# A graph layer on one core: second-phase table picks from three bf16 parts in 25 quads of 56 steps, own projections kept in DRAM, and 32 steps of rows issued by SyncE

## What is computed

```python
h = jnp.maximum(_layernorm(x), 0.0)
feat = relu(h @ W_pool + b_pool)
w = edge_weight / segment_sum(edge_weight, dst)[dst]
neigh = segment_max(feat[src] * w[:, None], dst)
rst = h @ W1_self + neigh @ W1_neigh + b1
h1 = relu(rst / norm(rst))
neigh2 = segment_sum(h1[src] * w[:, None], dst) / deg[:, None]
out = x + relu(h1 @ W2_self + neigh2 @ W2_neigh + b2)
```

## Time and profile before

| | |
|---|---|
| median of 3 runs | 3998.56 us (3998.48 to 3999.13) |
| the profiled execution | 3995.4 us |
| its span, first to last instruction | 3993.7 us |
| POOL busy in the span | 2970.4 us (74%) |
| DVE busy | 3064.5 us (77%) |
| PE busy | 2828.0 us (71%) |
| ACT busy | 1384.0 us (35%) |
| first phase, first to last gather | 113.4 to 1882.9 us |
| second phase, first to last gather | 2030.4 to 3847.2 us |

### The profile page before, as it was taken

The page is one execution under the profiler, slowest core; times in us unless marked ns, Lnnn a source line. Parts: engine busy times, 40 slices in busy tenths (PEclk is TensorE's granted clock), DMA queues, the critical chain, the costliest instruction groups (busy, mean ns, idle before and its releaser), DMA issues. The chain is left out here.

```text
span 3993.7 us, 55758 instructions
## 1 busy us (share of the span) xinstructions
PE 2828.0 (71%) x8603; PEld 1440.9 (36%) x8603; DVE 3064.5 (77%) x5593; ACT 1384.0 (35%) x4000; POOL 2970.4 (74%) x3150
## 2 busy tenths in 40 slices
PE   3133332222199999993679999999999999998536
PEld 3033332212144444441434443334434343345324
DVE  6488888768589998884568888888889898874234
ACT  6344443333333333332433333333333333334310
POOL 7777777777767777776767777777777777777766
PEclk8555555555599999996579999999999999996555
DMA  7333334444433333333333333333333333333335
GB/s 207 92 108 111 114 115 129 128 128 118 138 119 111 121 120 112 115 117 109 98 92 117 114 115 116 115 119 110 114 117 111 121 110 121 110 107 106 116 115 149
DMA packets 226164, 469.73 MB, mean 118 GB/s; under 512 B 67234, under 2 KB 144164, under 8 KB 200964
## 3 DMA queue, kind: packets, MB, share of 16 engines
q0 software_dynamic: 100416, 205.90, 20.0%
q1 hardware_dynamic: 116676, 258.00, 18.0%
q10 hardware_dynamic: 8704, 2.25, 0.3%
HBM read 240.82 MB, written 225.06 MB: 117 GB/s over the span
## 5 line engine op out<-in xcount | busy, mean ns | idle before, releaser
L519 POOL DMA_INDIRECT G<-h_tab,SRC x1451 | 1369.2, 944 | 460.0 <-issue 322.4
L519 POOL DMA_INDIRECT G<-feat_tab,SRC x1399 | 1326.9, 948 | 443.9 <-issue 295.0
L867 DVE TENSOR_TENSOR CP<-pH,kc 128x1024 f32<-128x1024 f32 x1225 | 1494.3, 1220 | 113.0 <-PE pM L1025 61.0
L640 ACT ACTIVATE pT<-G,EW 128x128 f32<-128x128 f32 x1434 | 525.0, 370 | 1009.1 <-DMA G<-h_tab,SRC 340.6
L640 ACT ACTIVATE pM<-G,EW 128x128 f32<-128x128 f32 x1416 | 518.8, 371 | 1012.6 <-DMA G<-h_tab,SRC 319.8
L1000 PE MATMUL pH<-CP 128*128 128x98 bf16 x1563 | 144.3, 281 | 597.6 <-DVE CP L825 597.6
L1024 PE MATMUL pM<-CP,A 128*128 128x512 f32 x882 | 463.0, 607 | 63.0 <-DVE CP L867 60.8
L1025 PE MATMUL pM<-CP,A 128*128 128x512 f32 x882 | 454.6, 597 | 0.0
L810 DVE SCALAR_TENSOR_TENSOR S<-S,C,pT 128x128 f32<-128x128 f32 x782 | 269.8, 345 | 220.4 <-ACT pT L640 198.2
L1024 PE MATMUL pC<-CP,A 128*128 128x512 f32 x784 | 409.9, 605 | 38.4 <-DVE CP L867 36.9
L1025 PE MATMUL pC<-CP,A 128*128 128x512 f32 x784 | 404.1, 597 | 0.0
(11 more groups left out here) (149 smaller groups left out, 2896.2 us busy)
## 6 DMA issues: line engine op xcount, KB each, us to landing
scan<-S SPq DMA_DIRECT2D x97, 1032.0 KB
scan<-S SPq DMA_DIRECT2D x97, 1024.0 KB
GR<-feat_tab SPq DMA_DIRECT2D x3456, 0.5 KB
GR<-h_tab SPq DMA_DIRECT2D x3456, 0.5 KB
GA<-feat_tab ACTq DMA_DIRECT2D x2176, 0.5 KB
GA<-h_tab ACTq DMA_DIRECT2D x2176, 0.5 KB
G<-h_tab,SRC POOLq DMA_INDIRECT x1451
G<-feat_tab,SRC POOLq DMA_INDIRECT x1399
```

The lines of the kernel that those rows point to most:

```text
L519: pool.indirect_dma_start(out=dst, out_offset=None, in_=table, in_offset=bass.IndirectOffsetOnAxis(ap=idx, axis=0)).then_inc(s, 16)
L640: act.activation(scaled(t), v, ACT.Copy, scale=EW[:, t:t + 1]).then_inc(s_mul, 1)
L867: dve.tensor_tensor(OH[:, k % 2, :, :], pH[:, :].unsqueeze(1).to_broadcast([P, 2, 4 * P]), kc[:, 2 * j:2 * j + 2].unsqueeze(2).to_broadcas ...
```

## The change

- The second phase has 25 quads with windows of 56 steps, from step 76 on. The first phase keeps 8 quads with windows of 80 steps, one block later.
- For them the table is split at the start of the second phase into three bf16 parts, in 75 pieces, one in each of the steps 0 to 74: PE puts a group into PSUM, DVE rounds it to bf16, PE subtracts that part, and so on (`SPLIT`, `split`, `third`). Two parts take the place of the fp32 tile in A, the third lies in U and HL.
- A pick of the second phase is one DVE instruction with 1024 bf16 results (`pick_split`), compared with codes that are made once at the start and loaded as bf16, and six bf16 matmuls in place of two fp32 ones. Four one-hot buffers instead of two.
- The own projections run in the steps 120 to 1545. SP loads a group of `h_tab` (`load_nodes`), and stores the result to a new DRAM tensor (`store_own`); the last node stage reads it back (`load_own`).
- SP issues the rows of 32 steps in each phase, used one block later than before.

```diff
-QUADS = [(0, 54 + QB * i) for i in range(8)] + [(1, QB * i) for i in range(17)]
+SPL = 76
+Q1 = [(0, T * 55 + 80 * i, 80) for i in range(8)]
+Q2 = [(1, SPL + 56 * i, 56) for i in range(25)]
+QUADS = Q1 + Q2
+NHOT = 4
...
 def chunk_block(c):
-    return 7 * c // 16
+    return 3 * c // 8
...
-ROWT = [T * (chunk_block(CH * k + CH - 1) + 1) + 9 for k in range(27)]
+ROWT = [T * (chunk_block(CH * k + CH - 1) + 2) + 9 for k in range(32)]
...
+AHEAD = 16
+OWN_FIRST, OWN_EACH = 120, 57
+OWN = {OWN_FIRST + OWN_EACH * g: g for g in range(NGR + 1)}
...
+                    if phase:
+                        for g in range(NGR):
+                            if b == own_load_block(g):
+                                load_nodes(g)
+                            if b == own_store_block(g):
+                                store_own(g)
...
+            def pick_split(u, j, k):
+                if j == 0:
+                    arrived(dve, s_si, u)
+                    dve.wait_ge(s_o2, k)
+                    link(dve.tensor_copy(pH[:, :], SI[:, u % 2, :].bitcast(F32)))
+                dve.wait_ge(s_od, max(K1, k - NHOT + 1))
+                dve.tensor_scalar(HOT[:, k % NHOT, :], PH16[:, :], kcode[:, j:j + 1], None,
+                                  ALU.is_equal).then_inc(s_o2, 1)
...
+                    if phase:
+                        for i in range(2):
+                            hot = HOT[:, k % NHOT, 4 * P * i:4 * P * (i + 1)]
+                            v = 2 * j + i
+                            pe.matmul(picked(u), AB[:, v, 0, :], hot, start=(v == 0), stop=False)
+                            pe.matmul(picked(u), AB[:, v, 1, :], hot, start=False, stop=False)
+                            ins = pe.matmul(picked(u), low_tile(v), hot, start=False, stop=(v == NT - 1))
```

More of the change, by code:

```diff
@@ L43, in quad_mul @@
     return QUADS[u][0] * TS + quad_steps(u)[-1] + 1
-PICKS = {(phase, T * b + j * T * QB // NJ): [] for phase, b in QUADS for j in range(NJ)}
-for u, (phase, b) in enumerate(QUADS):
+PICKS = {(phase, t + j * n // NJ): [] for phase, t, n in QUADS for j in range(NJ)}
+for u, (phase, t, n) in enumerate(QUADS):
     for j in range(NJ):
[L49 to L52, removed]
+        PICKS[phase, t + j * n // NJ].append((u, j))
+STARTS = {(phase, t // T): u for u, (phase, t, n) in enumerate(QUADS)}
+TAKEN = {(phase, t + n + (3, 7)[phase]): u for u, (phase, t, n) in enumerate(QUADS)}
+READ = {(phase, t + n + (7, 11)[phase]): u for u, (phase, t, n) in enumerate(QUADS)}
+SPLIT = [(g, k) for r in range(0, NGR, 2) for k in range(3) for g in range(r, min(r + 2, NGR))]
+SPLIT_AT = {gk: n for n, gk in enumerate(SPLIT)}
+assert len(SPLIT) < SPL
 PAT = {(QUADS[u][0], t): (u, i) for u in range(QN) for i, t in enumerate(quad_steps(u))}
@@ L104 @@
 I32 = mybir.dt.int32
+TWO = 0x40000000
 U8 = mybir.dt.uint8
@@ L122, in hist_of, with own_load_block, own_store_block @@
     return [k for k in (2 * (b - H0), 2 * (b - H0) + 1) if 0 <= k < NB]
[L125 to L135, removed]
+AHEAD = 16
+OWN_FIRST, OWN_EACH = 120, 57
+OWN = {OWN_FIRST + OWN_EACH * g: g for g in range(NGR + 1)}
+assert max(OWN) + AHEAD < TS and OWN_FIRST > len(SPLIT) + AHEAD
+def own_load_block(g):
+    return (OWN_FIRST + OWN_EACH * g - AHEAD) // T - 2
+def own_store_block(g):
+    return (OWN_FIRST + OWN_EACH * (g + 1)) // T + 1
 def build(nc, x, src, srcq, srcr, dstx, ew, w_pool, b_pool, w1s, w1n, b1, w2s, w2n, b2, out):
@@ L142, in build @@
     scan2 = nc.dram_tensor("scan2", (EP, D), F32).ap()
+    owntab = nc.dram_tensor("own_tab", (NP, D), F32).ap()
+    codes = nc.dram_tensor("codes", (QN, 8 * P), BF16).ap()
     with ExitStack() as ctx:
@@ L320, in build @@
         s_pq = sem("s_pq")
+        s_qi = sem("s_qi")
+        s_qe = sem("s_qe")
+        s_qs = sem("s_qs")
+        s_sp = sem("s_sp")
+        s_sd = sem("s_sd")
+        s_ring = [sem(f"s_ring{i}") for i in range(3)]
+        s_os = [sem(f"s_os{i}") for i in range(3)]
         s_ost = [sem(f"s_ost{i}") for i in range(3)]
@@ L421, in _ @@
                 sp.dma_start(rows(feat, g), F[:, g % 3, 0:len(tiles_of(g)), :]).then_inc(s_fst[g % 3], 16)
+            sp.wait_ge(s_qe, 1)
+            sp.dma_start(codes, QB[0:QN, :]).then_inc(s_qs, 16)
             ahead = []
@@ L449, in store_blocks @@
                             load_feat(i)
-                    if (phase, b) == (0, QUADS[0][1] - 1):
+                    if (phase, b) == (0, QUADS[0][1] // T - 2):
                         load_sources(0)
@@ L942, in _ @@
                 combine(1, t)
+                if t < len(SPLIT):
+                    split(t)
                 for u, j in PICKS.get((1, t), ()):
@@ L1091, in project_own @@
                 ins.then_inc(s_qp, 1)
+            for n, (g, k) in enumerate(SPLIT):
+                o = in_quad(pR[g % 2], len(tiles_of(g)))
+                if k:
+                    pe.wait_ge(s_sd, SPLIT_AT[g, k - 1] + 1)
+                    pe.matmul(o, nident[:, :], third(g, k - 1), start=False, stop=True,
+                              skip_group_check=True).then_inc(s_sp, 1)
+                else:
+                    if g >= 2:
+                        pe.wait_ge(s_sd, SPLIT_AT[g - 2, 2] + 1)
+                    pe.matmul(o, ident[:, :], raw(g), start=True, stop=True).then_inc(s_sp, 1)
+            pe.wait_ge(s_sd, len(SPLIT))
             for t in range(TS):
```

97 lines of the change are left out of this document (82 added, 15 removed).

## The result

The changed kernel takes 4219.48 us, median of 4 runs (4218.37 to 4220.38), beside 3998.52 for the one before (3995.79 to 3999.13). The ratio is 1.0554, with an interval of 1.0536 to 1.0572: 5.5% slower. The profiled execution took 4219.15 us with a span of 4217.4.

A forecast was written before the change was run, and what follows sets the result against it. The prediction took POOL's gathers, 1.25 us each, to bound the kernel before, with SP taking over after the change. 3995.4 + 121 (first phase) + 103 (second phase) + 1 (last stage) = 4220 us, range 4150 to 4290.

The forecast's parts named there:

- The mechanism: Both phases: added rows raise SP to 19.3 us a block, above POOL's 17.8 and 18.1, so SP sets the pace; 0.82.
- The first phase: Blocks 1 to 95, 63 of three chunks and 32 of two, plus loads, on SP: phase ends near 2008 us, +121 us.
- The second phase: From its start, 60 three-chunk and 30 two-chunk blocks plus code loads and own transfers on SP: 1924 us, +103 us.
- The 0.8 for each own transfer: Second phase, SP's queue: 50 transfers of own groups at 0.8 us each, 40 us, bounds 20 and 55.
- The last stage: After the second phase: SP loads 25 more groups of 256 KB beside the last gathers, 1 us (0 to 5).
- DVE: Second-phase picks: a comparison takes 0.68 us, so a 56-step window needs 53 us of DVE under SP's 70.
- The rival of 250 us more: Second phase: DVE's comparisons run at one element a cycle, a window takes 80 us, not 70; time 4470 us; chance 0.04.
- PE: Second-phase picks: six matmuls take 1.28 us, a window 66.5 of 70 us, leaving PE 5% away from being the bound.
- Rival 1: POOL stays the bound, kernel faster at 3935 us; needs SP's second-phase block under 18.1 us, a chunk 7% cheaper; chance 0.06.
- Signs in the profile: Expected after: hardly any SP waits, blocks of 21.6 and 14.8 us, POOL waiting for ACT 100 us or more, comparisons 0.65-0.7 us.
- Rival 1's 17 us: First phase: up to 17 us of POOL stalls that the later use of the rows could remove, counted in Rival 1's time.
- The register loads: SP's loads of 16 offsets: costed at the profile row's 1.16 us minimum, 1.26 median, not the skill page's 600 ns floor.

The follow-up runs named there:

- Experiment 2: Kernel before with only SP's rows changed: 32 steps of rows in each phase, chunk pattern 3, 3, 2, used one block later; 4170.32 us.
- experiment 4: Changed kernel with the third table part left out of each second-phase pick, four matmuls instead of six; 4218.40 us.
- experiment 7: Kernel before with only its 27 steps of rows used one block later; 4001.27 us, ratio 0.9996.
- experiment 9: Kernel before with rows and first-phase quads both one block later, first source numbers loaded in the same block as before; 3979.62 us, ratio 0.9958.
- experiment 1: Changed kernel with SP's rows back to 27 steps in the old chunk pattern 2, 2, 3, still used a block later; 4050.23 us.
- experiment 3: Changed kernel with 32 offsets in one register load of SP instead of 16, row DMAs as many as before; 4138.24 us.
- experiment 5: Changed kernel with 27 steps of rows on SP and only two of three table parts in each second-phase pick; 3936.54 us.
- experiment 6: Changed kernel with 27 steps of rows on SP and 23 quads with windows of 60 steps instead of 25 with 56; 3956.71 us, ratio to before 0.9883.
- experiment 8: Changed kernel with 23 quads in windows of 60 steps, 30 steps of rows on SP, 32 offsets per load, chunk pattern 1, 1, 1, 2; 3976.58 us, ratio 0.9944.

## Why the prediction was right

It said 4220 us, with a range of 4150 to 4290 and 0.93 for slower; 4219.5 was measured.

- *The mechanism.* SP was to take over as the bound in both phases. Experiment 2 shows it for the rows alone, and experiment 4 shows that in the changed kernel SP needs no help from PE to make the time. What the prediction did not see is how near PE stands: DVE waits for PE through most of the second phase.
- *The first phase.* The store of block 0 was expected at 151.9 and stands at 153.0. The last block with rows was to end at 2004, and the stores behind it begin at 2004.32. The second phase starts 2152.44 - 2030.55 = 122 us later; the term was 121. Two errors offset in it. The blocks of two chunks with no load took 15.04 us (mean of 18), not 14.8, and a part of the table added 0.6 us (10 blocks), not the 1.1 that was read from one pair of blocks.
- *The second phase.* From 2152.44 to 4068.8 it takes 1916 us, where 1924 was expected: +95 instead of +103. Blocks 6 to 95 took 4065.6 - 2278.1 = 1787.5 us, where 1740 + 54 = 1794 had been summed. The 0.8 for each own transfer was not too high: a fit over the 89 blocks of SP's timeline gives 0.6 us for a load of nodes and 1.2 for a store of an own group, 0.9 on the mean, the store above my bound of 1.1. Too high was the block itself. 28 blocks of three chunks with nothing else took 21.04 to 21.76 us, mean 21.42, and 60 of them at 0.18 less than 21.6 are 11 us.
- *The last stage.* From the last store to the end it is 148.6 us, 6.5 more than before; I had taken 1, with bounds of 0 to 5. The term was too small. The runs tell a part of it: from the gather of the run correction (FR) to the end it is 137.6 to 138.6 us in the four profiles whose last stage is the old one (before, experiments 2, 7 and 9), and 140.8 to 142.3 in the seven with the own groups read back. So reading them back costs 3 to 4 us. Whether it is the loads or their place in SP's queue was not tried.
- The sum is 122 + 95 + 6.5 = 223.5 us, which is the difference of the spans. Errors of 8 us down and 5.5 up nearly cancel; that the total is off by only 1 us is luck, and a miss of some 8 us is what the terms would bear.
- *DVE.* A comparison takes 0.75 us (743 to 753 ns over all 1225), where I took 0.68. That is outside the 0.65 to 0.7 that was named as a sign. The Trainium skill, VectorE: DVE Perf Modes, section "The perf-mode tier table", allows such an operation with an operand in PSUM up to two elements a cycle. The trace agrees that it is more than one: at the clock of 0.96 GHz that the same page gives, one a cycle would be 1.07 us, an estimate from the page. The rival of 250 us more did not occur.
- *PE.* The timeline of the second phase has the first matmuls of two threes 0.65 us apart, and over ten threes from there it is 1.29 us for a pick (1.28 expected):

```profile
2699.73 0.38 PE L1140 MATMUL pM<-CP,A 128*128 128x512 bf16 x1
...
2700.38 0.38 PE L1140 MATMUL pM<-CP,A 128*128 128x512 bf16 x1
```

  The window was put at 66.5 us and is 68.1 (3.5 blocks at PE's pace). I had called PE 5% away from SP; it is 2% away. Had SP been faster by more, PE would have taken over, and the change would still have been slower than before, as experiment 1 shows with 4050 us. Rival 1, the only way to "faster", needed more than the cheaper chunk that I named for it: with SP relieved PE was waiting behind it. Its 7% was also reckoned without the own transfers; from 19.9 us a block to 18.1 it is 9% of the block. Its chance of 0.06 should have been smaller still.
- *Signs in the profile.* SP's missing waits, the block times, the counts and POOL's waits for ACT (255 and 272 us, where 100 or more were named) came as written. Beside DVE's comparison one more sign did not: ACT's longest waits were to be for SP's rows. They are for DVE:

```profile
ACT pT L712 <- DVE S L898: 494.9, 175, 15.2
ACT pT L712 <- DVE S L895: 252.0, 91, 18.7
ACT pT L712 <- DMA GR<-feat_tab: 154.0, 24, 8.4
```

ACT waits in most cases for DVE to free the PSUM slots. DVE in turn waits 152.4 us for stores of SP in the first phase, and in the second for PE and at its end for stores; the late rows are only part of the way by which SP holds the others.

- *Rival 1's 17 us* of stalls in the first phase were put down to the later use of the rows. Experiments 7 and 9 show that the rows alone do not do it, and that with the quads' shift, which the change has too, 17.6 us go.
- *The register loads.* The Trainium skill, DMA: Bandwidth & Descriptors, section "Latency and other measured facts", gives a floor of about 600 ns. No load of 16 registers on SP came near it (1.14 us at least in the changed kernel), and by experiment 3 it is 0.34 us and 0.0575 for each register; the prediction was right to go by the row.

## What to carry to other kernels

An engine that only issues DMAs has no busy share, so measure its work from one of its periodic instructions to the next, in a stretch where it does not wait, and multiply before giving it more. When a chain names one engine as the bound, look for a second one with no waits: here cutting the work of the engine that the chain named by a third gained nothing, cutting the other's gained 169 us of 221, most of it in the phase where the first was no bound, and only both together made the kernel faster than before. Balance by the narrowest stretch of a phase and not by its mean.

## What the runs showed of the hardware

- A register load on SP's queue took 1.26 us for 16 registers and 2.18 us for 32, which is 0.34 us and 0.0575 for each register by these two points.
- Issuing one row of 512 bytes from SP takes 0.32 us from one to the next: ten rows stand in 3.12 us of SP's timeline, in before and after alike.
- PE was busy without a break for 1000 us of products, most of them bf16, at a granted clock of 0.99 (experiment 1). In the run with a third of the picks' products removed, with PE 77% busy, the granted clock was 0.89 on the mean (experiment 4).
- POOL's gathers stood 1.249 us apart in undisturbed stretches of before, after and experiments 5, 6, 8 and 9, and 1.251 us in experiments 1 to 4 and 7, with median durations of 944 or 945 and 947 ns. Over the 2850 gathers of the kernel before that is an estimated 6 us. What makes the difference stays open.
